# Routed and shared feed-forward with head-diagonal attention on one core: the choice of experts in parts of 4, 4, 8 and 16 tiles, and two weight steps moved to accumulating DMAs

## What is computed

```python
# attention over the 16 sequences, 16 heads of 8 channels
q, k, v = (einsum('cthd,ed->cthe', xn_heads, W) for W in (Wq, Wk, Wv))
diag = einsum('cthd,cthd->cth', q, k) / sqrt(128)
attn = softmax(diag, axis=0)[..., None] * v.sum(axis=1)[:, None]
# routed feed-forward: 16 experts, the best two of each token
scores = softmax(xn @ gate_w + gate_b); top_vals, top_idx = top_k(scores, 2)
cw = (one_hot(top_idx, 16) * top_vals[..., None]).sum(axis=1)
y = sum over e of cw[:, e] * ((silu(xn @ w1[e] + b1[e]) * (xn @ w3[e] + b3[e])) @ w2[e] + b2[e])
# shared feed-forward, 352 wide
z = (silu(xn @ sw1 + sb1) * (xn @ sw3 + sb3)) @ sw2 + sb2
out = x + attn + y + z
```

## Time and profile before

| | |
|---|---|
| median of 3 runs | 285.69 us (284.89 to 286.25) |
| profiled execution, its own time | 287.19 us |
| span in the profile | 285.4 us |
| mean granted TensorE clock | 0.949 |
| busy: PE, DVE, POOL, ACT | 222.3, 174.0, 153.1, 112.8 us |

### The profile page before, as it was taken

One profiled execution on the slowest core, in us unless ns is written; L12 is line 12 of the kernel. 1 busy time (PEld: TensorE's weight loads), 2 busy tenths in 40 slices (PEclk: granted clock), 3 DMA queues, 4 the chain that ended last, 5 costly groups with the idle time before them and its releaser, 6 DMA issues.

```text
span 285.4 us, 4839 instructions
## 1 busy us (share of the span) xinstructions
PE 222.3 (78%) x1303; PEld 171.4 (60%) x1303; DVE 174.0 (61%) x497; ACT 112.8 (40%) x336; POOL 153.1 (54%) x171
## 2 busy tenths in 40 slices
PE   8989993999799789849877888787687778876700
PEld 6655772645675353548766776676676667765500
DVE  5998737688577489814535545553554555544486
ACT  2378743031207205204534534443453444533400
POOL 6335676767666667711554564555455545555530
PEclk9999988899979999968999999999999999999965
DMA  7999211113446321100232232222222475462238
GB/s 205 346 409 256 88 53 44 52 52 105 122 132 225 91 75 52 54 21 0 70 89 72 78 88 80 79 70 84 74 81 78 135 225 167 100 200 67 94 114 281
DMA packets 27580, 33.57 MB, mean 118 GB/s; under 512 B 4819, under 2 KB 23507, under 8 KB 27203
## 3 DMA queue, kind: packets, MB, share of 16 engines
q1 hardware_dynamic: 20788, 21.28, 26.2%
q0 software_dynamic: 4576, 9.91, 10.3%
q10 hardware_dynamic: 2192, 2.10, 2.2%
HBM read 18.94 MB, written 14.33 MB: 117 GB/s over the span
## 4 chain that ended last, share of the span: by engine, by line
PE 60%; DVE 23%; another core or an unknown queue 8%; issue 4%; ACT 2%; DMA 1%; SPq 0%; DVEq 0%
PE PS L1122 16%; PE PS L1101 14%; PE PS L974 5%; PE PS L942 4%; PE PS L941 4%; PE PS L1110 3%; DVE fw L731 3%; PE PS L1111 3%; PE PS L1091 3%; DVE rxl L723 3%; DVE XR L446 2%; PE PS L910 2%; DVE X L744 2%; DVE X L742 2%
## 5 line engine op out<-in xcount | busy, mean ns | idle before, releaser
L419 POOL DMA_INDIRECT ydram<-fw x79 | 76.3, 965 | 76.1 <-DVE fw L731 52.2
L410 POOL DMA_INDIRECT xslot<-XR,idx x64 | 62.4, 975 | 33.7 <-issue 16.9
L1101 PE MATMUL PS<-w13h,rxh 128*128 x79 | 32.6, 412 | 25.5 <-DVE rxl L723 24.1
L731 DVE TENSOR_SCALAR fw<-PS,fw 128x128 f32<-128x128 f32 x79 | 27.6, 349 | 39.9 <-PE PS L1122 36.2
L1122 PE MATMUL PS<-fw 89*128 (+1 forms) x316 | 50.2, 281 | 1.2 <-ACT fw L878 1.0
L1122 PEld LDWEIGHTS PS<-fw 89*128 89x128 f32 (+1 forms) x316 | 41.3, 190 | 4.4 <-issue 3.6
L870 ACT ACTIVATE rxh<-PS 128x128 fp32r<-128x128 f32 x79 | 22.0, 278 | 55.2 <-PE PS L1091 42.3
L727 DVE TENSOR_TENSOR prod<-prod,PS 128x176 f32<-128x176 f32 x79 | 26.7, 338 | 25.1 <-ACT prod L874 13.9
L974 PE MATMUL PS<-sw,sS 128*128 128x128 f32 (+1 forms) x192 | 28.7, 318 | 12.4 <-DVE X L588 4.7
L974 PEld LDWEIGHTS PS<-sw,sS 128*128 128x128 f32 (+1 forms) x192 | 27.8, 232 | 15.7 <-issue 10.2
L874 ACT ACTIVATE prod<-PS 128x176 f32<-128x176 f32 x79 | 24.9, 316 | 25.4 <-PE PS L1101 15.7
(11 more groups left out here) (139 smaller groups left out, 330.1 us busy)
## 6 DMA issues: line engine op xcount, KB each, us to landing
fw<-xslot SPq DMA_DIRECT2D x79, 72.0 KB
fw<-in_w SPq DMA_DIRECT2D x1, 2816.0 KB, 17.4
X<-in_x SPq DMA_DIRECT2D x8, 256.0 KB, 6.3
XR<-ydram SPq DMA_DIRECT2D x4, 512.0 KB
out<-X ACTq DMA_DIRECT2D x7, 256.0 KB, 2.6
fw<-in_w SPq DMA_DIRECT2D x1, 1536.0 KB
xnT<-ydram SPq DMA_DIRECT2D x3, 512.0 KB, 3.9
ydram<-fw POOLq DMA_INDIRECT x79
```

The costliest lines, as they stand in the source:

```text
L410: pool.indirect_dma_start(xslot, bass.IndirectOffsetOnAxis(ap=idx[:, k, t:t + 1], axis=0), XR[:, t, :], None).then_inc(d_sc[k][h][q], 16)
L419: pool.indirect_dma_start(ydram, bass.IndirectOffsetOnAxis(ap=RX[:, v, TOK:TOK + 1].bitcast(I32), axis=0), yb[:, v, :], None).then_inc(d_y ...
L731: dve.tensor_scalar(yb[:, v, :], PS[:, 6 + b, 0:P], RX[:, v, CWT:CWT + 1], None, ALU.mult).then_inc(r_y, 1)
L1101: ins = pe.matmul(PS[:, 2 + b, 0:F2], x[:, b, :], w[:, bass.ds(e * F2, F2)], start=(k == 0), stop=(k == 2))
```

## The change

- The choice is made in four parts (`SEG`) of 4, 4, 8 and 16 tiles, with the 12 operations as single functions that are listed one by one among other work; `index` runs per part and choice, and POOL sends by units of 4, 4, 8, 8 and 8 tiles (`UNIT`, `dispatch`). The paced waits are gone.
- Groups 1, 4, 5, 6 and 7 are normalised by ACT (`BY_ACT`, scale and bias with a new row of products `nmr`), the others by DVE; POOL does none.
- `fold`, its constants and `split` are gone. The host rolls `w13` by one row. POOL negates the left-out row, SP stores it to DRAM (`ndram`), and an accumulating DMA of POOL adds it to all 128 rows of `w13`. ACT writes `w13h` (`high`) and then its negative into `w13l` (`minus`), and a second accumulating DMA of POOL adds `w13` to that; it stands in POOL's list behind 40 of the 64 indirect DMAs. The row of the biases in `w13l` and the first tile loads wait for it (`d_low`).
- SP loads `w13` ahead of the x groups 4 to 7, and the constants in two pieces.
- The dense work is listed anew on all engines. `down(6)` and `down(7)` run inside the loop, at steps 3 and 5; until tile 6 the second transposes use one bank (`SOLO`, `ra_bank`), since the other one holds the dense result.
- At the end PE adds two of the 9 pieces by products with the identity, ACT copies them out, DVE does the other seven; the stores are reordered, and `DONE` has one more level. The block ends without a drain of POOL (`no_gpsimd_drain`).

```diff
-POOLED = (4, 5)
+BY_ACT = (1, 4, 5, 6, 7)
+BY_DVE = (0, 2, 3)
+SEG = ((0, 4), (4, 8), (8, 16), (16, 32))
+UNIT = (0, 4, 8, 16, 24, 32)
+TAIL_PE = (0, 1)
+TAIL_OUT = (2, 0, 3, 1, 4, 5, 6, 7, 8)
+SOLO = 6
-DONE = (HT, HT + 8, HT + 12, NT)
+DONE = (HT, HT + 8, HT + 12, HT + 14, NT)
...
@@ sync
+            sp.dma_start(row0[:], d["w13"][P - 1:P, :].rearrange("a (p w) -> (a p) w", p=P)).then_inc(l_r0, 16)
...
+            sp.wait_ge(k_neg, 1)
+            sp.dma_start(ndram.rearrange("a (p w) -> (a p) w", p=P), row0[:]).then_inc(d_neg, 16)
+            sp.dma_start(w13, d["w13"]).then_inc(l_w13, 16)
             for g in range(4, NG):
                 load_x(g)
...
-            sp.wait_ge(s_sm, 2 * NB)
+            sp.wait_ge(d_low, 16)
             sp.dma_start(w13l[WP:P, :].bitcast(F32), bdram[1:2, :]).then_inc(d_bup, 16)
...
-            sp.wait_ge(s_w, KEPT)
+            sp.wait_ge(d_low, 16)
             sp.wait_ge(s_em, 1)
             scattered(0)
@@ gpsimd
+            pool.wait_ge(l_w13, 16)
+            pool.wait_ge(d_neg, 16)
+            pool.dma_start(w13, ndram.to_broadcast([P, NE * F2]), accum_op=ALU.add, max_dma_last_dim=NE * F2).then_inc(d_fold, 16)
...
+            dispatch(0, 0)
+            dispatch(0, 1)
+            dispatch(1, 0)
+            dispatch(1, 1)
+            dispatch(0, 2)
+            dispatch(1, 2)
+            dispatch(0, 3)
+            pool.wait_ge(s_wn, NW)
+            pool.dma_start(w13l[:].bitcast(F32), w13, accum_op=ALU.add, max_dma_last_dim=NE * F2).then_inc(d_low, 16)
+            dispatch(0, 4)
+            dispatch(1, 3)
+            dispatch(1, 4)
@@ scalar
+            def norm(g):
+                act.wait_ge(s_nm, len({unit(o) for o in BY_ACT if unit(o) <= unit(g)}))
+                for t in range(g * GT, (g + 1) * GT):
+                    ins = act.activation(XR[:, t, 0:P], X[:, t, :], ACT.Identity, bias=nmr[:, t:t + 1], scale=rstd[:, t:t + 1])
+                ins.then_inc(s_xp, 1)
...
             def high(q):
-                act.wait_ge(s_w, q + 1)
-                act.activation(w13h[0:WP, q * WQ:(q + 1) * WQ], PS[0:WP, 5, 0:WQ], ACT.Copy).then_inc(s_wh, 1)
+                act.wait_ge(d_fold, 16)
+                act.activation(w13h[:, q * WQ:(q + 1) * WQ], w13[:, q * WQ:(q + 1) * WQ], ACT.Copy).then_inc(s_wh, 1)
+
+            def minus(q):
+                act.wait_ge(s_wh, q + 1)
+                if q == 0:
+                    act.wait_ge(s_sm, 2 * NB)
+                act.activation(w13l[:, q * WQ:(q + 1) * WQ], w13h[:, q * WQ:(q + 1) * WQ].bitcast(F32), ACT.Copy, scale=-1.0).then_inc(s_wn, 1)
@@ tensor
-            steps(run, {0: lambda: down(6), 1: lambda: down(7)})
+            steps(run, {3: lambda: down(6), 5: lambda: down(7)})
+
+            pe.wait_ge(r_xl, NS)
+            for n, i in enumerate(TAIL_PE):
+                c, w = TAIL[i]
+                pe.wait_ge(d_yl[i], 16)
+                at = PS[:, n, :].rearrange("p (t e) -> p t e", e=P)
+                pe.matmul(at, ident, X[:, c * CL:(c + w) * CL, :], start=True, stop=False)
+                pe.matmul(at, ident, landing(c, w)[:, :, 0, :], start=False, stop=False)
+                pe.matmul(at, ident, landing(c, w)[:, :, 1, :], start=False, stop=True).then_inc(r_f, 1)
```

More of the change, by code:

```diff
@@ L62 @@
 RAW = 8
+W0 = NE * F2 // P
 WP = P - 1
@@ L93, with unit @@
 NY = 2 * N + NZ * P
+def unit(g):
+    return sum(e <= g * GT for e in UNIT[1:])
 class Chain:
@@ new lines, in _ @@
+            invert(0)
+            norm(0)
+            stats(2)
+            stats(3)
+            invert(1)
+            peak(0)
+            shift(0)
+            tied(0)
+            invert(2)
+            top_rank(0)
+            top_mask(0)
+            strike(0)
+            peak2(0)
+            tied2(0)
+            ranks2(0)
+            low_rank(0)
+            low_mask(0)
+            both(0)
+            rank(0)
+            norm(2)
+            weigh(0)
+            peak(1)
+            shift(1)
@@ new lines, in _ @@
+            tied(1)
+            top_rank(1)
+            top_mask(1)
+            strike(1)
+            peak2(1)
+            tied2(1)
+            ranks2(1)
+            low_rank(1)
+            index(0, 0)
+            weigh(1)
+            stats(4)
+            low_mask(1)
+            both(1)
+            rank(1)
+            stats(5)
+            norm(3)
+            index(0, 1)
+            stats(6)
+            invert(3)
+            stats(7)
+            index(1, 0)
+            index(1, 1)
@@ new lines, in _ @@
+            gated(0, 0)
+            invert(4)
+            peak(2)
+            shift(2)
+            tied(2)
+            top_rank(2)
+            top_mask(2)
+            strike(2)
+            peak2(2)
+            tied2(2)
+            ranks2(2)
+            low_rank(2)
+            low_mask(2)
+            both(2)
+            rank(2)
+            index(1, 2)
+            weigh(2)
+            index(0, 2)
+            peak(3)
+            shift(3)
+            tied(3)
+            top_rank(3)
@@ L684, in _ @@
+            rank(3)
+            weigh(3)
+            gated_up(3, 0)
+            index(1, 3)
+            index(0, 3)
+            score(4)
+            tally(4)
+            score(5)
+            slot_table()
+            score(6)
+            slots()
+            tally(5)
+            gated_up(3, 1)
+            gated_up(3, 2)
+            add_z(1)
             tally(6)
             score(7)
+            add_z(2)
             tally(7)
+            gated_up(4, 0)
             shift_scores()
-            split(4)
+            gated_up(4, 1)
@@ L1033, in _ @@
-            ins.then_inc(s_tot, 1)
-            project(2)
             up(3, 1)
-            fold(1)
+            rank(3)
+            project(4)
+            project(5)
             up(3, 2)
-            fold(2)
+            totals()
+            project(6)
+            project(7)
+            table_rows()
+            down(2)
             up(4, 0)
-            project(3)
-            pe.wait_ge(s_sl, 1)
-            pe.matmul(PS[0:2, 4, LV * NE:LV * NE + NS], slf[:], ident[0:NS, 0:NS], start=True, stop=True).then_inc(s_slt, 1)
```

649 lines of the change are left out of this document (332 added, 317 removed).

## The result

The changed kernel takes **320.93 us** (median of 4 runs, 318.92 to 322.69); the kernel before, run beside it, 285.58. The ratio is **1.124** (95% interval 1.119 to 1.129). 269.2 was forecast, and 258 to 284. The profiled execution took 318.92 us, with a span of 317.1. In all tables here the time is the median of all executions of a run, while ratio and interval come from its fast executions alone, so that the two can differ a little.

A forecast was written before the change was run, and what follows sets the result against it. PE, busy 78% of the span, was taken as the bound. Stretches of 110.9 + 146.7 + 11.3 gave a span of 268.9 us, 16.5 less in own time, so 285.69 - 16.5 = 269.2 us; range 262 to 275, whole 258 to 284.

The forecast's parts named there:

- step *fold: Ahead of the loop: 11 products leave PE, 9.5 us less; POOL's waits on PE's progress go too, without a price.
- Vb: Ahead of the loop: the dense work reaches attend(0) at about 84, Vb comes at 87; plus 3 us, ends 0 and 5.
- D: Time of one accumulating DMA, early in the kernel: taken as 17.4 us, between 7 and 34.8, holding tile 1 until 105.
- R1: Rival: accumulating DMAs decide when tile 1 starts; up to 298 us. Chance 0.09 for the far part, 0.13 for the milder.
- down(6) and down(7): Moved from the loop's start into it: 11.7 us less ahead, 4.5 more in the loop, 1.5 more for the single bank.
- A: Stretch ahead of the loop, to the mark at 131.55 us: forecast to fall to 110.9 us.
- Choice in four parts: Ahead of the loop: wins part of PE's hole and slow calls around it, 4 us less, ends 0 and 7.6.
- R2: Rival: the choice is late, the dense chain waits and the clock falls; 120.4 us ahead of the loop, 279 total. Chance 0.14.
- B: The loop, from the mark at 131.55 us to the end's first addition: forecast to grow from 140.7 to 146.7 us.
- C: Stretch from the end's first addition to the end of the span: forecast to fall from 13.2 to 11.3 us.
- R3: Rival: the lists fit, the whole 7.6 us is won and the moved calls hide better in the loop; 260 us. Chance 0.14.
- R4: Rival: scatters end late and the loop runs dry at tile 12; 273 us if POOL is 18 us later. Chance 0.03.

The follow-up runs named there:

- f2: Kernel before with its four tables of paced waits emptied, first kind of chip: 327.9 us, ratio 1.148.
- e4: Changed kernel with the low part of w13 by 11 DVE subtractions instead of the second accumulating DMA, without paced waits: 324.9 us, ratio 1.143.
- h2: Changed kernel with the low part by DVE instead of the second accumulating DMA, and 13 paced waits, first kind of chip: 301.2 us, ratio 1.058.
- f1: The changed kernel itself, run again as a control on the first kind of chip: 316.1 us, ratio 1.108.
- f3: Changed kernel with 13 waits of POOL on PE's progress put between the scatters, first kind of chip: 312.5 us, ratio 1.100.
- e6: Changed kernel with 13 waits of POOL on PE's progress put between the scatters, second kind of chip: 254.1 us, no ratio given.
- e8: Changed kernel with the low part by DVE instead of the second accumulating DMA, and 13 paced waits, second kind of chip: 239.1 us, ratio 1.058.
- g2: Kernel before with down(6) and down(7) moved into the loop and the end of the change added, second kind of chip: 229.0 us, ratio 1.014.
- e7: Changed kernel with seven small POOL memsets, waiting only for each other, after each 4 scatters, second kind of chip: 252.0 us, ratio 1.114.
- h1: Kernel before with down(6) and down(7) moved into the loop, first kind of chip: 286.3 us, ratio 0.995.
- e5: Kernel before with its four tables of paced waits emptied, second kind of chip: 226.5 us, ratio 0.997.
- e3: Changed kernel with the first accumulating DMA (subtraction of the left-out row) left out, without paced waits: 310.5 us, ratio 1.092.
- f4: Changed kernel with 13 paced waits and both accumulating DMAs left out, first kind of chip: 294.4 us, no ratio given.
- g4: Changed kernel with 25 paced waits, both accumulations replaced by a plain broadcast load and DVE subtractions, second kind of chip: 252.3 us, ratio 1.106.
- e1: Changed kernel with both accumulating DMAs left out, without paced waits: 318.6 us, ratio 1.111.

## Why the prediction was wrong, point by point

**The waits that "go too" (step *fold*).** This is the step that failed. I wrote that the first scatter waited for PE's progress and not for an index, and that "these waits go too", and put them at nothing in the sum. On the first kind of chip they are what keeps the other engines on time. In the kernel before they are worth 42 us (f2), in the changed one 24 where the second accumulation is gone (e4 to h2), and 4 at most where it stays (f1 to f3), because the wait for `Vb` then takes their place. The waits and both accumulations together make 22 us of the changed kernel (316.1 to 294.4); no single edit gives them. I had seen the waits on PE and read them as a delay of POOL; I did not ask what an unbroken row of scatters does to the other engines. The trace of before had hints: ahead of the hole at 44 us DVE's `add_z` waits 6.0 us for a "remote" release and starts at 44.18, 1.9 us after a row of POOL's scatters has ended at 42.31, and the wait behind the 4.7 us of nothing after 120.5 ends at 124.39, 2.2 us after POOL's last scatter. I put the first down to DVE's list and did not ask about the second.

***Vb*.** Forecast at +3, with 0 to 5. With the waits back it is a wait of 19.4 us (f3), and the second accumulation costs 11 us (f3 to h2). On the second kind of chip it costs 15 by the medians (e6 to e8), but e6's executions reach from 6 to 18 us above e8's median. The term was priced without the accumulation that is issued ahead of `Vb`. Nor does the slot table come "at about the same time": the fills that wait for it begin at 86.46 where it was 65.52, and on the second kind at 72.09 in e8 where it was 58.20 in g2.

**The accumulating DMAs (D = 17.4).** The first took 21.4 us to landing, and the queueing that R1 assumed is there: the scatters issued behind it land only after it, POOL waits 9.6 us for them, and it comes to its first second choice at 40.5, where the prediction had 20 + D. The second was issued at 92.59; its landing isn't in this profile, and it took 20.2 us in e6 and 19.5 in e7. The row of the biases that waits for it was issued at 119.49, but that is no measure of it, since the row ahead of it in SP's list, which doesn't wait for it, went at 119.15. With 92.59 + 20.2 and the prediction's 5.8 us behind it, the two DMAs hold the tiles until 119; the third product came at 159. So R1 named the right direction and the wrong path: it had `d_low` decide, and that would have given a time near 277. The estimate worked out from the formula of the Trainium skill for a DMA from POOL (DMA: Bandwidth & Descriptors, "Anatomy of one DMA"), 8.6 us, is far from the 21.4 measured here for an accumulating one.

**down(6) and down(7): -11.7, and +4.5 + 1.5 with the single bank.** Read from the one profile of h1: -7.4 and +3.6. The loop's part was not more than forecast. In A the last `split` and a fallen clock came where the calls had been. On the second kind of chip it is -1.5 and +4.1, a loss.

**Choice in four parts: -4.** It was not a gain. In the cleanest comparison, on the second kind of chip and without the second accumulation, e8 has its third product at 118.93 and g2 (the choice in halves, all of `fold` on PE) at 107.55. Without `fold`'s 9.5 us e8 should be earlier. It stands 11.4 later, and the granted clock over 24 to 44 us is 0.57 against 0.91 in g2 and 1.00 in e5. First e8, then e5:

```profile
24.00:44.00 20.00, 16.20 (x75) 14.08 (x75) 10.91 (x47) 15.62 (x48) 7.97 (x10) 0.57 1.00 224
```

```profile
24.00:44.00 20.00, 19.43 (x121) 13.98 (x120) 17.37 (x44) 15.62 (x38) 11.81 (x13) 1.00 0.39 100
```

That is R2's sign (PE idle early, the clock at half), and some 21 us with `fold` counted, where R2 gave 9.5. The fallen clock belongs to the lists: over 24 to 44 us it is 0.59 in e3 and 0.62 in f4 as well, where the first accumulation is out. And f4, with the waits and without either accumulation, is still 8 us above the kernel before, where the forecast was 16 below. How many of the 21 us are the lists', and how many the first accumulation's, whose landing POOL's second choice waits for (10.8 us in e8), was not settled: g4 was to tell and didn't.

**The loop and the end.** B was forecast at 146.7 and is 145.4, C 11.3 and is 12.7; the prediction's own terms for C gave "11.5 at least". PE's products of the two moved `down`s are there (116.6 us busy for 108.6). R3 and R4 had no part.

**The chances.** Slower had 0.09, all of it R1's far part. No rival asked what a removed wait had been protecting. That case would have come from asking, of the one part of the change that only deletes, what runs on time because of it.

## What to carry to other kernels

A wait that looks like a delay of its own engine may be what keeps the others on time. Before a paced wait is deleted, empty its table alone and run that. A cost can hide behind a larger one, so an experiment that takes one cause away and finds nothing (e1) has not shown that cause to be free; it takes the pair. And a schedule tuned on one chip may be worth nothing on another, as these waits are: a version must be compared beside its parent on the same chip.

## What was not expected of the hardware

- Five chips fell into two kinds. On three the kernel before takes 285.5 to 287.2 us, on two 226.5 and 228.4, with the same durations of single instructions (0.96 us for an indirect DMA issue, 0.32 for a product of the loop). In the loop, 140.7 against 102.8 us, the difference is in when PE's results are seen by ACT and DVE.
- On the first kind these releases follow the end of POOL's DMA issues, by 0.85 us in the loop and by 2 to 5 us behind long rows of scatters. In f2 one release came while the row still ran, and PE and the SP queue were slow too. That an unbroken row costs 42 us there and nothing on the other kind is shown (f2, e5); that POOL's issuing itself holds the others up is argued from these times. A run with pauses that depend on nothing, on the first kind, would settle it and was not had.
- An accumulating DMA of 2816 KB took 20.1 to 21.4 us to landing early in the kernel (lowest e8, highest the changed kernel), and 20.2 and 19.5 later on (e6, e7). The plain load of the same size took 10.5 to 12.1 in the changed kernel and its versions (lowest e4, highest g4).
